# Two gathers ahead or four: the edge buffers of a graph kernel's last stage

## What is computed

```
h = maximum(layernorm(x), 0)
W = einsum('rb,bio->rio', comp, basis)          # 8 relations
h_all = einsum('ni,rio->nro', h, W)             # a row for each node and relation
msgs = h_all[src, edge_type]                    # a gather of 50000 rows of 256
agg = segment_sum(msgs, dst)                    # added up by target node
y = gelu(agg + h @ loop_w + h_bias + h)
x = x + layernorm(y) * ln_gamma + ln_beta
```

## Time and profile before

| | us |
|---|---|
| median of 3 runs (lowest, highest) | 1618.47 (1613.39, 1624.01) |
| the profiled execution | 1609.75 |
| its span, first to last instruction | 1607.9 |
| first and last gather of the last stage start at | 1017.5 and 1575.1 |

### The profile page before, as it was taken

One profiled execution on the slowest core, in us unless ns is written; L12 is line 12 of the kernel. 1 busy time (PEld: TensorE's weight loads), 2 busy tenths in 40 slices (PEclk: granted clock), 3 DMA queues, 4 the chain that ended last, 5 costly groups with the idle time before them and its releaser, 6 DMA issues. The chain is left out here.

```text
span 1607.9 us, 18550 instructions
## 1 busy us (share of the span) xinstructions
PE 1168.3 (73%) x5463; PEld 864.7 (54%) x5463; DVE 908.4 (56%) x2801; ACT 454.6 (28%) x1150; POOL 889.5 (55%) x959
## 2 busy tenths in 40 slices
PE   5874579999899989999899988354565645553662
PEld 2443466777667766777667755233344424442452
DVE  5664577767777777777777662113434324533534
ACT  4652134443444443453444433000000000000000
POOL 2655656555555455555555510566676667666760
PEclk9997799999999999999999999687777767776776
DMA  6648666666667666566666611233343334433431
GB/s 203 157 132 265 208 200 201 205 222 202 207 197 233 206 210 188 189 223 189 203 191 220 194 46 57 79 108 106 113 125 114 114 106 121 119 115 109 121 114 51
DMA packets 137073, 255.68 MB, mean 159 GB/s; under 512 B 40426, under 2 KB 85460, under 8 KB 134026
## 3 DMA queue, kind: packets, MB, share of 16 engines
q0 software_dynamic: 50176, 154.19, 32.3%
q1 hardware_dynamic: 85834, 99.10, 19.0%
q10 hardware_dynamic: 960, 1.18, 0.2%
HBM read 192.76 MB, written 61.63 MB: 158 GB/s over the span
## 5 line engine op out<-in xcount | busy, mean ns | idle before, releaser
L1093 POOL DMA_INDIRECT arena<-qv_tab,srcs x392 | 391.8, 999 | 349.1 <-PE ps L1289 252.1
L1687 POOL DMA_INDIRECT arena<-h_all,typs x392 | 377.2, 962 | 210.3 <-issue 135.2
L1751 PE MATMUL ps<-arena 128*128 128x256 f32 x784 | 252.7, 482 | 114.8 <-DMA arena<-h_all,typs 49.9
L1289 PE MATMUL ps<-arena 128*128 128x264 f32 x784 | 221.2, 406 | 88.8 <-DVE arena L1437 49.9
L1751 PEld LDWEIGHTS ps<-arena 128*128 128x128 f32 x784 | 186.6, 246 | 176.1 <-issue 40.6
L1289 PEld LDWEIGHTS ps<-arena 128*128 128x128 f32 x784 | 140.2, 194 | 139.3 <-DVE arena L1437 66.8
L1500 DVE TENSOR_TENSOR arena<-arena,ps 128x512 f32<-128x512 f32 x196 | 134.3, 685 | 119.5 <-PE ps L1278 91.5
L1344 PE MATMUL ps<-wrel,arena 128*128 128x512 f32 x400 | 188.7, 598 | 1.7 <-ACT arena L1182 1.7
L1278 PE MATMUL ps<-arena 128*128 128x264 bf16 x1176 | 169.6, 282 | 12.6 <-DMA arena<-k_tab 11.0
L1278 PEld LDWEIGHTS ps<-arena 128*128 128x128 bf16 x1176 | 145.0, 145 | 41.4 <-issue 25.3
L1437 DVE TENSOR_TENSOR arena<-arena 128x512 f32<-128x512 f32 x196 | 134.0, 684 | 41.6 <-ACT arena L1150 40.9
(11 more groups left out here) (162 smaller groups left out, 1521.1 us busy)
## 6 DMA issues: line engine op xcount, KB each, us to landing
h_all<-arena SPq DMA_DIRECT2D x23, 1024.0 KB
arena<-dst SPq DMA_DIRECT2D x49, 256.0 KB
rel<-arena SPq DMA_DIRECT2D x77, 128.0 KB
arena<-k_tab SPq DMA_DIRECT2D x49, 198.0 KB
att<-arena SPq DMA_DIRECT2D x52, 132.0 KB, 6.0
qv_tab<-arena SPq DMA_DIRECT2D x25, 256.0 KB, 3.1
arena<-qv_tab,srcs POOLq DMA_INDIRECT x392
arena<-h_all,typs POOLq DMA_INDIRECT x392
```

Of the source, the lines that this page charges most:

```text
L1093: pool.indirect_dma_start(out=rowbuf[:, u * T + t, 0:2 * D], out_offset=None, in_=qv_tab, in_offset=bass.IndirectOffsetOnAxis(ap=srcs[:, v ...
L1289: last = nc.tensor.matmul(ps[:, AGG, 0:AW], ind[:, v % 2, t, :], rowbuf[:, v % 2 * T + t, D:2 * D + H], start=(t == 0), stop=(v == 0 and t ...
L1687: pool.indirect_dma_start(out=rowbuf[:, u * T + t, :], out_offset=None, in_=h_all[0:N * R, :], in_offset=bass.IndirectOffsetOnAxis(ap=typs ...
L1751: last = nc.tensor.matmul(ps[:, 6 + u, 0:D], ind[:, u, t, :], rowbuf[:, u * T + t, :], start=(t == 0), stop=(v == 0 and t == T - 1))
```

## The change

The buffers become four visits deep (`DEEP = 4`): 32 slots of `rowbuf`, four sets of indicators, `dl` and `car`, four `osum`, and banks 4 to 7 of PSUM. Each wait that was for visit v - 2 is for visit v - 4: POOL's for `agg_done`, DVE's and PE's for `osum_ready`, ACT's for the store. So no wait of these four stands in the first four visits, before in the first two alone. The landing semaphores of the rows become 16; eight are those of the attention stage used on, which is why `landed_of` adds what these have counted. The order of instructions on every engine stays. PE's `carry` still waits for `take` of the visit before, SP still stores one visit after the other, and a block's rest still stands between the indicators of an odd visit and of the next even one.

```diff
+DEEP = 4
-            rowbuf = cut([2 * T, D])
-            ind = cut([2, T, WIN])
-            dl = cut([2, T])
-            car = cut([2, WIN])
-            osum = cut([2, D])
-            row_in = [sem(f"messages_in{j}") for j in range(2 * PAIRS)]
+            rowbuf = cut([DEEP * T, D])
+            ind = cut([DEEP, T, WIN])
+            dl = cut([DEEP, T])
+            car = cut([DEEP, WIN])
+            osum = cut([DEEP, D])
+            row_in = row_in + [sem(f"messages_in{j}") for j in range(2 * PAIRS)]
+
+            def landed_of(v):
+                used = 32 * len(range(v % DEEP, G, 2)) if v % DEEP < 2 else 0
+                return used + 32 * (v // DEEP) + 32
+            SUMS = 8 - DEEP
...
                 for v in range(G):
-                    u = v % 2
+                    u = v % DEEP
                     for t in range(T):
-                        if t % 2 == 0 and v >= 2:
-                            pool.wait_ge(agg_done, PAIRS * (v - 2) + t // 2 + 1)
+                        if t % 2 == 0 and v >= DEEP:
+                            pool.wait_ge(agg_done, PAIRS * (v - DEEP) + t // 2 + 1)
...
                 def take(v):
                     act.wait_ge(win_done, v + 1)
-                    if v >= 2:
-                        act.wait_ge(rel_out, 16 * (v - 1))
-                    nc.scalar.activation(osum[:, v % 2, :], ps[:, 6 + v % 2, 0:D], ACT.Copy).then_inc(osum_ready, 1)
+                    if v >= DEEP:
+                        act.wait_ge(rel_out, 16 * (v - DEEP + 1))
+                    nc.scalar.activation(osum[:, v % DEEP, :], ps[:, SUMS + v % DEEP, 0:D], ACT.Copy).then_inc(osum_ready, 1)
...
                 def add_up(v):
-                    u = v % 2
+                    u = v % DEEP
                     pe.wait_ge(ind_ready, v + 1)
-                    if v >= 2:
-                        pe.wait_ge(osum_ready, v - 1)
+                    if v >= DEEP:
+                        pe.wait_ge(osum_ready, v - DEEP + 1)
...
-                            pe.wait_ge(row_in[u * PAIRS + t // 2], 32 * (v // 2) + 32)
+                            pe.wait_ge(row_in[u * PAIRS + t // 2], landed_of(v))
...
                 def indicators(v):
-                    u = v % 2
-                    if v >= 2:
-                        dve.wait_ge(osum_ready, v - 1)
+                    u = v % DEEP
+                    if v >= DEEP:
+                        dve.wait_ge(osum_ready, v - DEEP + 1)
```

More of the change, by code:

```diff
@@ L1649, in store @@
                         sp.wait_ge(rel_out, 16 * v)
-                    sp.dma_start(rel[bass.ds(w, WIN), :], osum[:, v % 2, :]).then_inc(rel_out, 16)
+                    sp.dma_start(rel[bass.ds(w, WIN), :], osum[:, v % DEEP, :]).then_inc(rel_out, 16)
                 def load_block(m, stores):
@@ L1743, in add_up @@
                 def add_up(v):
-                    u = v % 2
+                    u = v % DEEP
                     pe.wait_ge(ind_ready, v + 1)
-                    if v >= 2:
-                        pe.wait_ge(osum_ready, v - 1)
+                    if v >= DEEP:
+                        pe.wait_ge(osum_ready, v - DEEP + 1)
                     for t in range(T):
                         if t % 2 == 0:
-                            pe.wait_ge(row_in[u * PAIRS + t // 2], 32 * (v // 2) + 32)
-                        last = nc.tensor.matmul(ps[:, 6 + u, 0:D], ind[:, u, t, :], rowbuf[:, u * T + t, :],
+                            pe.wait_ge(row_in[u * PAIRS + t // 2], landed_of(v))
+                        last = nc.tensor.matmul(ps[:, SUMS + u, 0:D], ind[:, u, t, :], rowbuf[:, u * T + t, :],
                                                 start=(t == 0), stop=(v == 0 and t == T - 1))
@@ L1762, in carry @@
                     pe.wait_ge(car_ready, v)
-                    nc.tensor.matmul(ps[:, 6 + v % 2, 0:D], car[:, v % 2, :], osum[:, 1 - v % 2, :],
+                    nc.tensor.matmul(ps[:, SUMS + v % DEEP, 0:D], car[:, v % DEEP, :], osum[:, (v - 1) % DEEP, :],
                                      start=False, stop=True).then_inc(win_done, 1)
```

## The result

| | before | changed |
|---|---|---|
| median of 7 runs, us | 1618.96 | 1631.17 |
| lowest, highest | 1613.39, 1624.01 | 1625.82, 1634.26 |
| profiled execution | 1609.75 | 1629.17 |
| its span | 1607.9 | 1627.2 |

The ratio is 1.0076 with a 95% interval of 1.0057 to 1.0095. So the deeper buffers cost 9 to 15 us, 12.2 by the medians. That is real, and less than the 1% within which the prediction called it no change.

What follows compares the result with a forecast made beforehand. POOL's gather issue was taken as the floor, 492 of the last stage's 590 us, with stops and the end on top. Terms -3.0 + 16.0 - 6 = +7 us, put on the median 1618.47, gave 1625 us, range 1583 to 1643.

Steps and rivals of the forecast that it cites:

- The late reports: Last stage: PE's reports arrive late while POOL issues without a break, the rest together 3 to 4 us after it stops.
- The rhythm is kept: Last stage: POOL still stops 2.9 us after every 16 gathers despite the lead of four; 0 us, chance 0.46.
- The pair at the end: After the last gather: one more pair of visits is left for the chain, +16.0 us, bounds 8 and 23.1.
- POOL's lead at the start: Start of last stage: first stop at gather 49 at the earliest, before at 33; 16 gathers quicker, -3.0 us.
- the slow rival: Last stage: chain starves longer in the longer first unbroken run, +7, with the end pair +23 us, 1641; chance 0.19.
- Rows ready sooner: PE's waits for gathered rows, at most 28.7 us in 30 waits, go; two stops of 3 us saved, -6 us.
- its two wrong terms: POOL's lead at the start, -3.0 us, and rows ready before PE wants them, -6 us.

Runs made afterwards that it cites:

- the imposed one: In every second visit ACT's copy waits for landed rows, and POOL for that copy: kernel before 1630.37 us (1.0078), changed kernel 1642.91 us (1.016).
- the two halves, rows or sums: From the changed kernel, only rowbuf four deep: 1510.17 us (1.0003); only indicators, sums and PSUM banks four deep: 1509.24 us (1.0007).
- the two gated kernels: ACT's copy in every second visit held until POOL's semaphore increment, four extra copies added: kernel before 1508.7 us (0.9994), changed kernel 1515.78 us (1.0046).

## Why the prediction was right, and which of its terms were not

- **The late reports.** They are there, on late chips: in the changed kernel the nameless waits are 311.9 and 178.0 us; on a prompt chip the same program has reports within 0.05 us and POOL has no stop. The prediction read more into the earlier trace rows: only PE's reports, and all of them 3 to 4 us into a stop. The copy at 1047.60 in its own came with POOL unbroken, and in the changed kernel 11 of 37 late copies came in a stop; DVE's reports are late as well. What it built on this, that POOL's stops end with a late report and not with a free slot, held: 68.4 us of POOL's idle time have no named source, 9.7 end with PE. That it would be absent on other chips was not foreseen. What makes it on the chips that have it is not known.
- **The rhythm is kept (term 0 of 0 to -64).** Held. The stops stand at 68 us; from the 165th gather on they come 16 to 20 gathers apart and last 2.8 to 3.7 us, idle gap included. No run here varies the reports and keeps the depth on a late chip, so that the stops stay because of the late reports is the reading that fits, and not shown by an experiment of its own. The rule of the Trainium skill that spoke for the change (page Perfetto Trace Analysis, Identifying Performance Opportunities: a gap that repeats can mean too little SBUF or PSUM for the next tile) did not hold here: there are 64 us of stops with two visits and 68 with four. Where the chain was slow by itself, the stops did go with depth, as by the rule, and the time stayed at 1542.1.
- **The pair at the end (+16.0).** 16.1 in the profiled pair, 15.9 in the imposed one: the main term, read from the earlier trace rows and right. The lead of four was there when POOL was done.
- **POOL's lead at the start (-3.0).** Not obtained. The first stop came before the 53rd gather, as was said (none before the 49th), and the run was at 1.254 us a gather. But three stops followed within five gathers, 9.5 us in sum, and the stretch from the first to the last gather is 1.9 us longer, not 3 shorter. This looks like the slow rival's mechanism, a chain that starves longer in the first run; the rival's working gave +7 for it, and the stretch shows +1.9. The sign that the prediction gave for this rival, stops of 60 us or more and 15 more after the last gather, was met (68 and 16.1). But the forecast's own 55 to 65 us and its pair at the end meet it too, so it separates the two badly. It is one profiled execution, so I call it likely and not shown. In the imposed pair, where the stops are fixed, the same stretch is 1.9 shorter.
- **Rows ready sooner (-6).** The waits fell as forecast, from 28.7 us in 30 times to 5.8 in 9 beside the first one. They gave nothing. That they lay beside the late reports and not ahead of them is the likely reason. The prediction had written down that most of it is off the path, and took two stops all the same; the bound of 0 was the right value.
- **The sum.** +7 was forecast. The medians say +12.2, with 9 to 15 as the interval; the two terms that came to nothing make 9, and 16 alone would be just above the interval. That the forecast came out near is in part luck: its two wrong terms took 9 us off, and, for a reason that is not known, the medians lie 7 us less apart than the profiled pair. The profiled pair, 19.3 apart, is not a better figure: the profiled execution of before is 9.2 below its median, that of after 2.0 below. Where the other executions have the 4 to 7 us back isn't seen, since they have no trace. The predicted time of 1625 is 6 us short.
- **What the profile was to show.** Last gather at 1567 to 1575: it is 1578.3. Stops of 55 to 65 us: 68. 45 to 50 us after the last gather: 48. The other points came as written.

Left open: which of the two halves, rows or sums, carries the cost on a late chip, since both were run on a prompt one; whether fewer reports would help there; and why the stages ahead of the last one take some 32 us less on a prompt chip (the first gather starts at 986.7 and not 1018.8). There too the late chip has waits without a named source, 42.2 us of ACT, DVE and POOL in the changed kernel, and the prompt one has none. No version here is faster than the kernel before on its chip.

## What to carry to other kernels

Before a buffer is made deeper, look at what ends the stop of the engine that fills it. Where it ended with a late report, the depth left the stops as they were (64 and 68 us) and added its own length at the end. Where the consumer was the bound, it took the stops away (13.6 us to under 2) and gave no time. And when the last stage is short, count what is in store as work that is still to be done when the filler is through: two visits more were 16 us.

## What the runs showed of the hardware

- The kernel before took 1508 to 1510 us on four chips, and 1619 on another and where the result was measured. The last stage, from its first gather to the end, is 519 us in one and 608 in the other for the changed kernel. On the late chip a copy started up to 36.9 us after the matmul that it waited for in the changed kernel, 17.6 before, and 6.3 and 5.5 us in the mean of 48 copies; on a prompt one 0.04, always. After POOL's last gather the changed kernel's next copy was 4.3 us late, and the last three 0.04.
- An indirect gather of 128 rows of 1 KB keeps POOL for 0.95 us, and the next starts 0.30 us later, on either kind of chip: 1.25 to 1.27 us each, and no run here went below 1.25.
- A semaphore increment in POOL's list that stands behind indirect DMAs came twelve gathers before the last of them was issued, by the traces of the two gated kernels (ten at the very end, two deep). It is no mark of how far the gathers are.
- PE's granted clock in the last stage was 0.71 in the changed kernel on the late chip and 0.79 on the prompt one; with 14 products more a visit it was at 1.00 between 1020 and 1490 us, where PE was busy for 466.7 of the 470 us. The median matmul of the sums took 379 ns in the changed kernel on the late chip and 454 on the prompt one, so slower matmuls are not what makes the stage longer on the late chip.
